# First cross attention: the keys' squares rounded and split by GpSimd, summed by two bf16 matmuls, and taken ahead of the exponential on ScalarE

## The chip, the core and the metric

The kernel runs on one core of a Trainium2 chip. The metric is device time in microseconds of one execution of the whole program, as the median of several runs. The core's engines are TensorE (PE, with PEld for its weight loads), VectorE (DVE), ScalarE (ACT), GpSimd (POOL) and SyncE (SP, which here issues DMAs). Each has its own queue of instructions and runs it in order; semaphores tie the queues together.

## The reference, cut to what matters

The program is a decoder of two layers with a self attention, a cross attention and a feed-forward part each, and a layer norm behind every part. The change touches the cross attention of the first layer only (2 batches, 512 queries and 1024 keys each, 16 heads of 128, model width 512, context width 256):

```python
def _L0_xattn_ref(hidden_states, encoder_hidden_states, Wq, Wk, Wv, Wo, gq, gk):
    def rmsnorm(x, g, eps=1e-05):
        var = jnp.mean(jnp.square(x), axis=-1, keepdims=True)
        return x * jax.lax.rsqrt(var + eps) * g
    q = (hidden_states @ Wq).reshape(B, Sq, H, D)
    k = (encoder_hidden_states @ Wk).reshape(B, Skv, H, D)
    v = (encoder_hidden_states @ Wv).reshape(B, Skv, H, D)
    q = rmsnorm(q, gq)
    k = rmsnorm(k, gk)
    scores = jnp.einsum('bqhd,bkhd->bhqk', q, k) * scale
    attn = jax.nn.softmax(scores, axis=-1)
    out = jnp.einsum('bhqk,bkhd->bqhd', attn, v)
    return out.reshape(B, Sq, H * D) @ Wo
```

The part in question is the sum of a key's 128 squares inside `rmsnorm(k, gk)`.

## The kernel before

All products are float32 in effect: each operand is held as a bf16 high part and a bf16 remainder (hi and lo), and `three` (L1270) multiplies hi by hi, hi by lo and lo by hi into one bank of PSUM. These are the matmuls of L1272, L1273 and L1274 in the profile, whatever they compute; their tiles tell them apart (`k,q` are the scores, `wo,v` the product of probabilities and values, `cT,wkv` with 512 columns the keys, `xT,wq` the queries, `wkv,cT` with 128 columns the values). The transposed probabilities lie in memory that later holds the output weights, so the trace calls them `wo`.

Each attention runs over 32 units, a unit being one head of one batch, and a unit over QT = 4 tiles of 128 queries, in the order of `unit` on each engine. For a tile, TensorE (L1424) makes the scores, then the tile's jobs for the next unit, and then weighs the values for the tile three behind (LAG, L39). VectorE (L1209) scales the scores and finds their maximum (L1191), and later writes the remainder of the normalised probabilities (`remainder`, L1206). ScalarE (L883) writes the rounded probabilities of the tile before (`rounded`, L881), the negated maximum (L890), and the exponential (L892). SP transposes both parts by DMA (L467, L470).

The jobs prepare queries, keys and values of the next unit. Their plan is written out by hand in `Layer.jobs` (L71):

```python
plan = [[("K", 0)], [("KN", 0), ("K", 1)], [("KN", 1), ("Q", 0)], [("QN", 0), ("V", 0), ("V", 1)]]
```

K is a product of half the keys (512 of them), KN the sum of that half's squares, Q the queries, QN the sums of their squares, V half the values. In `job` (L1379) they take turns in two banks of PSUM, so each waits until VectorE is through with the job before the last (`job_lo`, L1384). On ScalarE `job_parts` (L821) takes a K out of PSUM twice behind the tile's exponential: squares into `sq` (L836), then the high part of the scaled keys into `k_hi` (L842). VectorE's part of a K is the low part `k_lo` (L1149), of a KN the scaled sum in `rk` (L1137). KN on TensorE (L1404) is one float32 multiplication of a matrix of ones with `sq`, which the trace shows as two matmuls; it waits for `sq_ok`. `key_norms` (L846) turns the sums into reciprocal roots at the end of the third tile.

GpSimd raises the query norms to the power -1/2 (L651) and splits weights into high and low parts, `split_hi` (L551) and `split_lo` (L556): in units with n % 4 of 2 or 3 the next heads' weights, in the last three units the output weights (`split_wo`). The latter's DMAs wait on SP until earlier pieces are split.

This layer's units are unrolled. Ahead of unit 0 the jobs of "unit -1" run alone, each step waiting for the one before.

Of the kernel before, what the change touches and what calls it, by code (L numbers as in the profile page):

```python
# [23 lines left out]
ALU = mybir.AluOpType  # L24
ACT = mybir.ActivationFunctionType
# [99 lines left out]
def build(nc, a, out, kept):  # L125
    ctx = ExitStack()
    with ctx:
# [19 lines left out]
        rstd = sb("rstd", [P, NT], F32)  # L147
        half_neg = sb("half_neg", [P, QT], F32)
        ones = sb("ones", [P, P], F32)
        idx = sb("idx", [P, IT], I32)  # L150

        q_max, q_inv, q_up, q_scale = (sb(x, [P, 48], F32) for x in ("q_max", "q_inv", "q_up", "q_scale"))
# [31 lines left out]
        t_amax, t_scaled, t_sum, qt_ok, qt_mm, qt_T = (sem(x) for x in ("t_amax", "t_scaled", "t_sum", "qt_ok", "qt_mm", "qt_T"))  # L184
        fg_mm, fu_mm, g_ok, u_ok, fs_ok, fy_ok = (sem(x) for x in ("fg_mm", "fu_mm", "g_ok", "u_ok", "fs_ok", "fy_ok"))

        idb_ok = sem("idb_ok")
        row_in = [sem(f"row_in{i}") for i in range(11)]

        by_name = {L.name: L for L in LAYERS}  # L190
# [65 lines left out]
        for li, L in enumerate(stages):  # L256
# [41 lines left out]
                m["rot"], m["swap"] = sb("rot", [P, 2, S], F32, s), sb("swap", [P, 2, S], F32, s)  # L298
            if L.rms:
                m["sq"] = sb("sq", [P, S], F32, s)  # L300
                m["rk"] = sb("rk", [P, 2, SC], F32, s)
                m["nq"] = sb("nq", [P, 2, QT], F32, s)
                m["g"] = sb("g", [P, 2], F32, s)
                m["mx"] = sb("mx", [P, 2], F32, s)
                m["gg"] = sb("gg", [P, 1], F32, s)
# [223 lines left out]
        def _(pool):  # L529
# [16 lines left out]
            nc.gpsimd.memset(ones[:, :], 1.0).then_inc(const_ok, 1)  # L546
            pool.wait_ge(const_ok, 4)
            nc.gpsimd.tensor_scalar(idb[:, :], ident[:, :], 1.0, 1.0, ALU.mult, ALU.mult).then_inc(idb_ok, 1)

            def split_hi(hi, src):  # L550
                nc.gpsimd.tensor_scalar(hi, src, 1.0, 1.0, ALU.mult, ALU.mult).then_inc(w_hi, 1)  # L551
# [53 lines left out]
            for li, L in enumerate(stages):  # L605
# [39 lines left out]
                def query_norms(n, it, qt, jobs):  # L645

                    for x, (kind, _) in enumerate(jobs):
                        if kind == "QN":
                            pool.wait_ge(job_lo, at(lambda n: c["lo"] + L.before(n, qt) + x + 1, n, it))
                            r = m["nq"][:, (n + 1) % 2, :]  # L650
                            nc.gpsimd.tensor_tensor(r, r, half_neg[:, 0:QT], ALU.pow).then_inc(q_norm, 1)  # L651

                def rope(n, it, qt, jobs):
                    for x, (kind, _) in enumerate(jobs):
                        if kind not in ("K", "Q"):
                            continue
                        r = ("Q", "K").index(kind)
                        hi = lambda n: c["hi"] + L.before(n, qt, BY_ACT) + x + 1
                        lo = lambda n: c["lo"] + L.before(n, qt) + x + 1
                        pool.wait_ge(job_hi, at(hi, n, it))  # L660
                        nc.gpsimd.tensor_tensor(m["swap"][:, r, :], m["swap"][:, r, :], m["sin"][:, :], ALU.mult).then_inc(rope_mul, 1)
                        pool.wait_ge(rope_mul, at(lambda n: c["rope"] + L.rope_count(n, qt) + 1, n, it))
                        pool.wait_ge(job_lo, at(lo, n, it))
                        nc.gpsimd.tensor_tensor(m["rot"][:, r, :], m["rot"][:, r, :], m["swap"][:, r, :], ALU.add).then_inc(rope_sum, 1)
# [6 lines left out]
                def unit(n, it):  # L671
                    for qt in range(QT):
                        if L.rope and qt:
                            rope(n, it, qt, L.jobs(n, qt))
                        if L.rms:
                            query_norms(n, it, qt, L.jobs(n, qt))
                        j, pieces = L.split_plan(n, qt)
                        for kind, part in pieces:
                            if part == 0:
                                pool.wait_ge(w_in[j], at(lambda n: c[f"win{j}"] + (32 if j == 0 or not L.gqa else 16) * (n // 4 + 2), n, it))  # L680
                                pool.wait_ge(job_mm, at(lambda n: c["job"] + L.before(n), n, it))
                                pool.nop(nofuse=True)
                            qkv_piece(L, kind, j, part, at(lambda n: c["whi"] + qkv_item(L, kind, j, n // 4 + 1), n, it))
                        if L.rope and qt == 0:
                            rope(n, it, qt, L.jobs(n, qt))
                        k = QT * (n - UNITS + 3) + qt - 1
                        if 0 <= k < 8:
                            split_wo(k)

                for n in (-2, -1):  # L690
                    for qt in range(QT):
                        if L.rope:
                            rope(n, None, qt, L.jobs(n, qt))
                        if L.rms:
                            query_norms(n, None, qt, L.jobs(n, qt))
                units(pool, unit, L)

# [24 lines left out]
        def _(act):  # L722
# [31 lines left out]
            for li, L in enumerate(stages):  # L754
# [34 lines left out]
                if names[li] == "ffn1":  # L789
# [28 lines left out]
                        turned_rows(t)  # L818
                    continue

                def job_parts(n, it, qt, jobs):  # L821
                    b, u = L.batch(n + 1), n + 1
                    for x, (kind, half) in enumerate(jobs):
# [4 lines left out]
                        if kind == "V":  # L828
                            nc.scalar.activation(m["v"][0][:, L.kvslot(u), 4 * half:4 * half + 4, :], bank.rearrange("p (t d) -> p t d", d=HD), ACT.Copy).then_inc(job_hi, 1)
                        elif L.rope:  # L830
                            r = ("Q", "K").index(kind)
                            nc.scalar.activation(m["swap"][0:64, r, :], bank[64:128, :], ACT.Copy)
                            nc.scalar.activation(m["swap"][64:128, r, :], bank[0:64, :], ACT.Copy).then_inc(job_hi, 1)
                        else:
                            if L.rms:
                                nc.scalar.activation(m["sq"][:, :], bank, ACT.Square).then_inc(sq_ok, 1)  # L836
                            if kind == "Q":
                                nc.scalar.activation(m["q"][0][:, u % 2, :], bank, ACT.Copy).then_inc(job_hi, 1)
                            else:
                                o = m["k"][0][:, L.kvslot(u), half * 512:half * 512 + 512]  # L840
                                if L.rms:
                                    nc.scalar.activation(o, bank, ACT.Copy, scale=m["gg"][:, 0:1]).then_inc(job_hi, 1)  # L842
                                else:
                                    nc.scalar.activation(o, bank, ACT.Copy).then_inc(job_hi, 1)
# [38 lines left out]
                def unit(n, it):  # L883
                    for qt in range(QT):
                        if n or qt:
                            rounded(*((n, it, qt - 1) if qt else (n - 1, it, QT - 1)))
                        act.wait_ge(s_max, at(lambda n: CREDIT + c["s"] + QT * n + qt + 1, n, it))
                        prob = m["p"][:, qt % 2, 0:L.width(qt)]
                        if L.rms:
# [16 lines left out]
                    act.wait_ge(const_ok, 7)  # L906
                for n in (-2, -1):
                    for qt in range(QT):
                        job_parts(n, None, qt, L.jobs(n, qt))
                        if L.rope and (n == -2 or qt == 0):  # L910
                            rotated(n, None, qt)
                        if L.rms:
                            key_norms(n, None, qt, L.jobs(n, qt))
# [355 lines left out]
        def _(pe):  # L1269
# [26 lines left out]
            for li, L in enumerate(stages):  # L1296
# [82 lines left out]
                def job(n, it, qt, x, kind, half):  # L1379
# [20 lines left out]
                            for ch in range(L.chunks):  # L1400
                                last = three(bank[:, t * P:t * P + P], lambda k: src[k][:, ch, o:o + P], lambda k: w(k, 1, ch), ch == 0, ch == L.chunks - 1)
                    elif kind == "KN":
                        pe.wait_ge(sq_ok, at(lambda n: c["sq"] + 3 * (n + 1) + half + 1, n, it))
                        last = nc.tensor.matmul(bank, ones[:, :], m["sq"][:, :], start=True, stop=True)  # L1404
                    elif kind == "QN":
                        pe.wait_ge(sq_ok, at(lambda n: c["sq"] + 3 * (n + 1) + 3, n, it))
                        for q in range(QT):
# [142 lines left out]
```

## Time and profile before

| | us |
|---|---|
| median of 3 runs (2616.11 to 2622.53) | 2621.8 |
| the profiled execution | 2614.38 |
| its span, first to last instruction | 2612.6 |
| TensorE busy | 2438.2 (93%) |
| VectorE busy | 1848.3 (71%) |
| ScalarE busy | 1588.8 (61%) |
| GpSimd busy | 711.8 (27%) |

Busy time counts an engine's instructions from start to end; matmuls overlap one another, so the step from the start of one kind of work to the start of the next says more than their durations. In a timeline the first number is the start in us from the start of the span, the second the duration, then engine, line, operation, tiles written and read, shapes, and in brackets how long the engine stood idle before it and what released it.

### The profile page before, as it was taken

The page shows a single profiled execution, that of the slowest core. Times are in us where ns is not written, and L with a number is a line of the kernel's source. Part 1 is how long each engine was busy: PE and PEld are TensorE (multiplying, and loading weights), DVE is VectorE, ACT ScalarE, POOL GpSimd, SP SyncE. Part 2 cuts the span into 40 slices and gives each one's busy share as a digit, 9 for nine tenths or more (in the row PEclk, how much of TensorE's full clock was granted, in tenths as well). Part 3 has the DMA queues.
Part 4 walks back from the last instruction along what each step waited for, and adds up shares of the span by engine and source line. Part 5 has one row for each costly group of instructions (what it writes and reads, how often), then busy time and mean ns, then how long its engine had stood idle before and what let it go on. Part 6 is the DMA issues. An engine that isn't in the chain of part 4 may idle for free. (4 is left out here: it accounts for less than half of the span.)

```text
span 2612.6 us, 57672 instructions
## 1 busy us (share of the span) xinstructions
PE 2438.2 (93%) x21584; PEld 1567.4 (60%) x21584; DVE 1848.3 (71%) x3371; ACT 1588.8 (61%) x2718; POOL 711.8 (27%) x671
## 2 busy tenths in 40 slices
PE   7999998989999999999988999999899999999864
PEld 4555555546666666666465666665566666665432
DVE  4777777657777777776665666667578888884597
ACT  5777675158887777886244566553277777773242
POOL 5666665601111111012332222226100000013111
PEclk9999999999999999999988999999999999999987
DMA  2433335325666666667341444445188777777200
GB/s 93 90 76 87 79 82 127 103 55 108 114 118 110 113 109 117 115 108 154 113 169 26 94 93 96 95 93 139 30 146 149 145 147 144 146 149 153 69 1 32
DMA packets 769429, 273.83 MB, mean 105 GB/s; under 512 B 737905, under 2 KB 740721, under 8 KB 767601
## 3 DMA queue, kind: packets, MB, share of 16 engines
q1 hardware_dynamic: 767504, 265.82, 49.0%
q0 software_dynamic: 1760, 5.77, 0.8%
q8 instruction: 110, 1.80, 0.3%
q14 instruction: 55, 0.44, 0.1%
HBM read 84.55 MB, written 6.44 MB: 35 GB/s over the span
## 5 line engine op out<-in xcount | busy, mean ns | idle before, releaser
L881 ACT ACTIVATE phl<-p,ri 128x1024 bf16<-128x1024 f32 (+4 forms) x512 | 437.4, 854 | 414.0 <-DVE ri L1196 386.1
L1206 DVE SCALAR_TENSOR_TENSOR phl<-p,ri,phl 128x1024 bf16<-128x1024 f32 (+4 forms) x512 | 514.1, 1004 | 103.3 <-issue 75.3
L892 ACT ACTIVATE p<-p,nb 128x1024 f32<-128x1024 f32 (+4 forms) x512 | 435.9, 851 | 53.9 <-DVE nb L1189 39.6
L1273 PE MATMUL ps<-wo_lo,v_hi 128*128 128x128 bf16 x2496 | 440.0, 220 | 0.0
L1272 PE MATMUL ps<-wo_hi,v_hi 128*128 128x128 bf16 x2240 | 396.5, 220 | 23.0 <-DMA wo_hi<-phl 15.7
L1274 PE MATMUL ps<-wo_hi,v_lo 128*128 128x128 bf16 x2240 | 396.2, 220 | 0.0
L1272 PE MATMUL ps<-k_hi,q_hi 128*128 128x512 bf16 (+3 forms) x768 | 272.5, 355 | 20.9 <-DVE nb L1187 18.7
L1273 PE MATMUL ps<-k_lo,q_hi 128*128 128x512 bf16 (+3 forms) x768 | 271.9, 354 | 0.0
L1274 PE MATMUL ps<-k_hi,q_lo 128*128 128x512 bf16 (+3 forms) x768 | 271.7, 354 | 0.0
L1273 PEld LDWEIGHTS ps<-wo_lo,v_hi 128*128 128x128 bf16 x2496 | 245.1, 98 | 33.4 <-issue 0.5
L1272 PEld LDWEIGHTS ps<-wo_hi,v_hi 128*128 128x128 bf16 x2240 | 219.5, 98 | 68.0 <-DMA wo_hi<-phl 27.9
L551 POOL TENSOR_SCALAR wkv_hi<-raw_kv 128x1024 bf16<-128x1024 f32 (+1 forms) x56 | 49.2, 878 | 658.9 <-PE ps L1274 509.5
L1274 PEld LDWEIGHTS ps<-wo_hi,v_lo 128*128 128x128 bf16 x2240 | 219.7, 98 | 0.0
L1272 PE MATMUL ps<-xT_hi,wq_hi 128*128 128x512 bf16 x512 | 195.1, 381 | 4.5 <-DVE xT_lo L958 3.5
L1191 DVE CUSTOM_DVE_ANT_0 p<-ps,rk,nq 128x1024 f32<-128x1024 f32 x128 | 163.1, 1274 | 51.3 <-PE ps L1274 51.0
L1273 PE MATMUL ps<-xT_lo,wq_hi 128*128 128x512 bf16 x512 | 195.1, 381 | 0.0
L1274 PE MATMUL ps<-xT_hi,wq_lo 128*128 128x512 bf16 x512 | 195.1, 381 | 0.0
L1272 PE MATMUL ps<-wo_hi,oT_hi 128*128 128x512 bf16 x512 | 194.4, 380 | 0.6 <-DVE nb L1187 0.6
L1273 PE MATMUL ps<-wo_lo,oT_hi 128*128 128x512 bf16 x512 | 194.2, 379 | 0.0
L1274 PE MATMUL ps<-wo_hi,oT_lo 128*128 128x512 bf16 x512 | 194.1, 379 | 0.0
L651 POOL TENSOR_TENSOR nq<-nq,half_neg 128x4 f32<-128x4 f32 x32 | 32.3, 1010 | 549.6 <-DVE nq L1140 549.6
L1189 DVE CUSTOM_DVE_ANT_0 p<-ps,mb 128x1024 f32<-128x1024 f32 x128 | 155.8, 1217 | 36.5 <-PE ps L1274 34.2
(200 smaller groups left out, 6126.5 us busy)
## 6 DMA issues: line engine op xcount, KB each, us to landing
raw_kv<-in_wkvself SPq DMA_DIRECT2D x32, 512.0 KB, 4.0
raw_q<-in_wqself SPq DMA_DIRECT2D x32, 256.0 KB, 2.6
raw_q<-in_woself SPq DMA_DIRECT2D x32, 256.0 KB, 2.8
raw_q<-in_wqcross SPq DMA_DIRECT2D x32, 256.0 KB, 3.0
raw_q<-in_wocross SPq DMA_DIRECT2D x32, 256.0 KB, 3.0
wo_hi<-phl SPq DMA_TRANSPOSE x384, 3.2
wo_lo<-phl SPq DMA_TRANSPOSE x384, 3.1
raw_kv<-in_wkvcross SPq DMA_DIRECT2D x24, 256.0 KB, 3.2
```

The source lines that it names most:

```text
L551: nc.gpsimd.tensor_scalar(hi, src, 1.0, 1.0, ALU.mult, ALU.mult).then_inc(w_hi, 1)
L651: nc.gpsimd.tensor_tensor(r, r, half_neg[:, 0:QT], ALU.pow).then_inc(q_norm, 1)
L881: nc.scalar.activation(m["ph"](qt, w), m["p"][:, qt % 2, 0:w], ACT.Copy, scale=ri[:, qt % 2:qt % 2 + 1]).then_inc(p_norm, 1)
L892: nc.scalar.activation(prob, prob, ACT.Exp, scale=1.0 if L.rms else -1.0, bias=nb[:, qt % 2:qt % 2 + 1], accum_out=rs[:, qt % 2:qt % 2 + 1 ...
L1189: ins = nc.vector.tensor_tensor_reduce(in1=m["mb"][:, L.batch(n), :], scale=-ISQ, op0=ALU.add, **kw)
L1191: ins = nc.vector.tensor_tensor_reduce(in1=m["rk"][:, n % 2, :], scale=m["nq"][:, n % 2, qt:qt + 1], op0=ALU.mult, **kw)
L1206: nc.vector.scalar_tensor_tensor(out=m["pl"](qt, w), in0=m["p"][:, qt % 2, 0:w], scalar=ri[:, qt % 2:qt % 2 + 1], in1=m["ph"](qt, w), op0= ...
L1272: nc.tensor.matmul(o, l(0), r(0), start=first, stop=False)
L1273: nc.tensor.matmul(o, l(0), r(1), start=False, stop=False)
L1274: return nc.tensor.matmul(o, l(1), r(0), start=False, stop=last)
```

## The change

ScalarE: the squares of the keys move from `job_parts`, behind the exponential, to a new `key_squares` ahead of the wait for the maximum. GpSimd: a new `squares` rounds `sq` to bf16 (`sqh`) and subtracts to get the remainder (`sql`), in the tiles that have a K, ahead of its other work in that tile. TensorE: KN waits for `sq_lo` and makes two bf16 matmuls with bf16 ones. The squares of the queries stay behind the exponential and now also wait for `sq_lo`.

```diff
@@ build: semaphores and buffers
+        onesb = sb("onesb", [P, P], BF16)
+        idb_ok, onesb_ok = sem("idb_ok"), sem("onesb_ok")
+        sq_hi, sq_lo = sem("sq_hi"), sem("sq_lo")
+                m["sqh"], m["sql"] = sb("sqh", [P, S], BF16, s), sb("sql", [P, S], BF16, s)
@@ GpSimd
+            nc.gpsimd.tensor_scalar(onesb[:, :], ones[:, :], 1.0, 1.0, ALU.mult, ALU.mult).then_inc(onesb_ok, 1)
+                def squares(n, it, qt, jobs):
+                    for kind, half in jobs:
+                        if kind == "K":
+                            pool.wait_ge(sq_ok, at(lambda n: 3 * (n + 1) + half + 1, n, it))
+                            if half:
+                                pool.wait_ge(job_mm, at(lambda n: c["job"] + L.before(n, 1) + 1, n, it))
+                            elif n >= 0:
+                                pool.wait_ge(job_mm, at(lambda n: c["job"] + L.before(n - 1, 2) + 1, n, it))
+                            nc.gpsimd.tensor_scalar(m["sqh"][:, :], m["sq"][:, :], 1.0, 1.0, ALU.mult, ALU.mult).then_inc(sq_hi, 1)
+                            pool.wait_ge(sq_hi, at(lambda n: 2 * (n + 1) + half + 1, n, it))
+                            nc.gpsimd.tensor_tensor(m["sql"][:, :], m["sq"][:, :], m["sqh"][:, :], ALU.subtract).then_inc(sq_lo, 1)
@@ GpSimd, unit and the units ahead of 0
                         if L.rms:
+                            squares(n, it, qt, L.jobs(n, qt))
                             query_norms(n, it, qt, L.jobs(n, qt))
@@ ScalarE
+                def key_squares(n, it, qt, jobs):
+                    for x, (kind, half) in enumerate(jobs):
+                        if kind == "K":
+                            act.wait_ge(job_mm, at(lambda n: c["job"] + L.before(n, qt) + x + 1, n, it))
+                            if n >= 0 or half:
+                                act.wait_ge(sq_lo, at(lambda n: 2 * (n + 1) + half, n, it))
+                            nc.scalar.activation(m["sq"][:, :], ps[:, M_BANK + (L.before(n, qt) + x) % 2, :], ACT.Square).then_inc(sq_ok, 1)
@@ ScalarE, job_parts
-                            if L.rms:
+                            if L.rms and kind == "Q":
+                                act.wait_ge(sq_lo, at(lambda n: 2 * (n + 1) + 2, n, it))
                                 nc.scalar.activation(m["sq"][:, :], bank, ACT.Square).then_inc(sq_ok, 1)
@@ ScalarE, unit
                             rounded(*((n, it, qt - 1) if qt else (n - 1, it, QT - 1)))
+                        if L.rms:
+                            key_squares(n, it, qt, L.jobs(n, qt))
                         act.wait_ge(s_max, at(lambda n: CREDIT + c["s"] + QT * n + qt + 1, n, it))
@@ ScalarE, the units ahead of 0
+                        if L.rms:
+                            key_squares(n, None, qt, L.jobs(n, qt))
                         job_parts(n, None, qt, L.jobs(n, qt))
@@ TensorE, job
                     elif kind == "KN":
-                        pe.wait_ge(sq_ok, at(lambda n: c["sq"] + 3 * (n + 1) + half + 1, n, it))
-                        last = nc.tensor.matmul(bank, ones[:, :], m["sq"][:, :], start=True, stop=True)
+                        pe.wait_ge(onesb_ok, 1)
+                        pe.wait_ge(sq_lo, at(lambda n: 2 * (n + 1) + half + 1, n, it))
+                        nc.tensor.matmul(bank, onesb[:, :], m["sqh"][:, :], start=True, stop=False)
+                        last = nc.tensor.matmul(bank, onesb[:, :], m["sql"][:, :], start=False, stop=True)
```

## Rows read from the trace of the kernel before

**Rows 1.** Busy time by stretch, one unit: stretch, its length, each engine's busy time, clock, DMA.

```profile
826.56:847.74 21.18, 21.09 (x207) 14.30 (x205) 15.70 (x26) 16.94 (x27) 2.02 (x3) 1.00 0.69 125
```

**Rows 2.** Who waited for whom, 560 to 1190 us: total, times, longest.

```profile
DVE k_lo L1149 <- ACT k_hi L842: 58.1, 59, 1.4
...
PEld ps L1272 <- DVE k_lo L1149: 41.6, 59, 1.0
```

**Rows 3.** Timeline of TensorE in that unit, first matmul of each kind of work.

```profile
827.85 0.38 PE L1272 MATMUL ps<-cT_hi,wkv_hi 128*128 128x512 bf16 x1
...
829.15 0.22 PE L1272 MATMUL ps<-wo_hi,v_hi 128*128 128x128 bf16 x1
...
831.78 1.02 PE L1404 MATMUL ps<-sq,ones 128*128 128x512 f32 x2
832.89 0.39 PE L1272 MATMUL ps<-cT_hi,wkv_hi 128*128 128x512 bf16 x1
...
836.84 1.02 PE L1404 MATMUL ps<-sq,ones 128*128 128x512 f32 x2
837.69 0.38 PE L1272 MATMUL ps<-xT_hi,wq_hi 128*128 128x512 bf16 x1
...
840.28 0.22 PE L1272 MATMUL ps<-wo_hi,v_hi 128*128 128x128 bf16 x1
```

**Rows 4.** Timeline of ScalarE in that unit.

```profile
829.52 0.20 ACT L890 ACTIVATE nb<-mx 128x1 f32<-128x1 f32 x1 [0.87 <-DVE mx L1191]
829.75 1.15 ACT L892 ACTIVATE p<-p,nb 128x1024 f32<-128x1024 f32 x1
...
830.90 0.57 ACT L836 ACTIVATE sq<-ps 128x512 f32<-128x512 f32 x1
831.38 0.68 ACT L842 ACTIVATE k_hi<-ps,gg 128x512 bf16<-128x512 f32 x1
...
840.48 0.60 ACT L836 ACTIVATE sq<-ps 128x512 f32<-128x512 f32 x1 [0.26 <-PE ps L1274]
```

**Rows 5.** Timeline of VectorE in that unit.

```profile
829.40 1.28 DVE L1206 SCALAR_TENSOR_TENSOR phl<-p,ri,phl 128x1024 bf16<-128x1024 f32 x1
832.09 0.75 DVE L1149 SCALAR_TENSOR_TENSOR k_lo<-ps,gg,k_hi 128x512 bf16<-128x512 f32 x1 [1.40 <-ACT k_hi L842]
...
834.24 1.28 DVE L1206 SCALAR_TENSOR_TENSOR phl<-p,ri,phl 128x1024 bf16<-128x1024 f32 x1
```

**Rows 6.** Timelines of GpSimd, VectorE and TensorE at places of this and the next stage.

```profile
1191.21 0.62 POOL L551 TENSOR_SCALAR wo_hi<-raw_q 128x512 bf16<-128x512 f32 x1 [4.09 <-DMA raw_q<-in_wocross]
...
1195.16 1.28 DVE L1206 SCALAR_TENSOR_TENSOR phl<-p,ri,phl 128x1024 bf16<-128x1024 f32 x1 [0.49 <-issue]
...
1195.60 1.32 POOL L551 TENSOR_SCALAR wo_hi<-raw_q 128x512 bf16<-128x512 f32 x1 [2.54 <-DMA raw_q<-in_wocross]
1197.01 1.16 POOL L556 TENSOR_TENSOR wo_lo<-raw_q,wo_hi 128x512 bf16<-128x512 f32 x1
...
1211.16 1.42 DVE L1206 SCALAR_TENSOR_TENSOR phl<-p,ri,phl 128x1024 bf16<-128x1024 f32 x1
...
1211.59 2.01 POOL L556 TENSOR_TENSOR wo_lo<-raw_q,wo_hi 128x512 bf16<-128x512 f32 x1
...
1327.42 6.17 POOL L625 TENSOR_TENSOR gu_lo<-oT_hi,gu_hi 128x2048 bf16<-128x2048 f32 x1 [14.94 <-ACT gu_hi L763]
...
1333.65 0.39 PE L1272 MATMUL ps<-xT_hi,gu_hi 128*128 128x256 bf16 x1 [4.99 <-POOL gu_lo L625]
```

**Rows 7.** Entry of the stage: busy time by stretch (as rows 1), then timelines.

```profile
535.00:545.25 10.25, 8.14 (x17) 2.40 (x17) 2.51 (x5) 3.19 (x5) 0.00 (x0) 0.62 0.01 2
...
538.15 0.60 ACT L836 ACTIVATE sq<-ps 128x512 f32<-128x512 f32 x1 [2.32 <-PE ps L1274]
...
538.90 2.04 PE L1404 MATMUL ps<-sq,ones 128*128 128x512 f32 x2 [0.84 <-ACT sq L836]
540.73 0.63 PE L1272 MATMUL ps<-cT_hi,wkv_hi 128*128 128x512 bf16 x1
...
545.25 0.39 PE L1272 MATMUL ps<-xT_hi,wq_hi 128*128 128x512 bf16 x1 [0.18 <-DVE k_lo L1149]
```

More of the change, by code:

```diff
@@ L185, in build @@
         fg_mm, fu_mm, g_ok, u_ok, fs_ok, fy_ok = (sem(x) for x in ("fg_mm", "fu_mm", "g_ok", "u_ok", "fs_ok", "fy_ok"))
-        idb_ok = sem("idb_ok")
+        idb_ok, onesb_ok = sem("idb_ok"), sem("onesb_ok")
+        sq_hi, sq_lo = sem("sq_hi"), sem("sq_lo")
         row_in = [sem(f"row_in{i}") for i in range(11)]
@@ L694, in _ @@
                         if L.rms:
+                            squares(n, None, qt, L.jobs(n, qt))
                             query_norms(n, None, qt, L.jobs(n, qt))
```

## The prediction, made before the changed kernel had run

> **What bounds the kernel now.** I read the busy shares by stretch first, then who waited for whom inside the first cross attention, then one unit of that stage (one head of one batch) engine by engine, then the places where GpSimd works beside VectorE, and last the entry of the stage. The unit that I follow lasts 21.18 us, from its first scores to the next unit's, and TensorE is busy for 21.09 of them (matmuls are pipelined, so a short wait hides in that figure), ScalarE 16.94, VectorE 15.70, GpSimd 2.02 [rows 1]. So TensorE looks like the whole bound. The waits say something finer: TensorE's weight loads stood 41.6 us, 59 times, on VectorE's low half of the keys (k_lo, L1149), and that operation in turn 58.1 us on ScalarE's high half (L842) [rows 2]. In TensorE's rows it is seen at the second key product: the sums of squares start at 831.78 and the next product only at 832.89, 1.11 later, while the second sums (836.84 to 837.69) take 0.85 [rows 3]. The 0.26 between is a wait for k_lo, which starts at 832.09 and lets TensorE go at 832.89, 0.80 later [rows 3, 5]. The second place, Q at 837.69, is held by TensorE itself by a small margin. TensorE and the loop of ScalarE and VectorE are therefore nearly equally long; an edit that shortens one and touches the other must be walked through both.
>
> **The parts, and the price of each.**
>
> Removed: 64 float32 sums (two matmuls each), 0.85 us of TensorE each [rows 3]. Added: 64 pairs of bf16 matmuls. A key product is six of them with 512 columns in 1.30 us (827.85 to 829.15 [rows 3]), so 0.22 each and 0.43 a pair. By itself that frees 0.42 x 2 = 0.84 us a unit, over 31 units and the entry 27 us: the most this change could ever give.
>
> Moved on ScalarE: the key squares now stand ahead of the exponential. A square starts 0.20 after TensorE turns to the next work (840.28 to 840.48), lasts 0.58 to 0.60, and the following operation starts 0.48 after it (830.90 to 831.38) [rows 3, 4]. First key half: TensorE leaves it at 829.15, so square 829.35, negated maximum 829.83 (before 829.52), exponential 0.23 later, 830.06, high keys 1.15 after that, 831.21 (before 831.38: the square now fills part of the idle time ahead of the maximum). k_lo follows 0.71 behind (831.38 to 832.09), at 831.92, and TensorE may start the second product at 832.72 [rows 4, 5].
>
> Added on GpSimd, which has room: a rounding of 128x512 took 0.62, a subtraction 1.16, the second starting 0.09 behind the first [rows 6]. Undisturbed, and with 0.08 for the hand-over from ScalarE too, that would be 829.93 + 0.08 + 0.62 + 0.09 + 1.16 = 831.88, just when TensorE is through its scores at 831.78. But it isn't undisturbed. VectorE's remainder (L1206, both inputs in SBUF) runs from 829.40 to 830.68 [rows 5]. Where GpSimd started within such an operation (1195.60, VectorE 1195.16 to 1196.44), its rounding took 1.32 in place of 0.62 and ended 0.48 behind VectorE; a subtraction at 1211.59 took 2.01 in place of 1.16, beside a remainder that itself took 1.42 in place of 1.28 [rows 6]. So the rounding ends at 830.68 + 0.48 = 831.16, the subtraction runs 831.25 to 832.41, and TensorE starts 0.06 later (a subtraction that ended at 1333.59 released it at 1333.65 [rows 6]), at 832.47. The pair ends at 832.90, and there the second key product starts: 0.01 later than before. The whole 0.42 that TensorE was given, and the 0.26 that it had waited, is spent waiting for GpSimd.
>
> A rule of the skill, in sentences of their own: the Trainium skill ("SBUF — State Buffer", Who interferes with whom) has GpSimd and a VectorE instruction with two SBUF inputs shut each other out for the whole instruction. By it GpSimd's full 0.62 would follow VectorE's end and not 0.48, 0.14 more a unit, 4.3 us over the stage.
>
> Second key half: product 832.90 to 834.20, square 834.40, maximum 834.88 (it could go earlier; ScalarE now waits for TensorE ahead of it), exponential 835.11, high keys 836.26, k_lo 836.97, and Q on TensorE 0.80 later at 837.77, against 837.69: 0.08 late. This step comes out of the order alone: from second product to Q it was 4.80, now it is 1.30 + 0.20 + 0.48 + 0.23 + 1.15 + 0.71 + 0.80 = 4.87. GpSimd here: the remainder stood 2.15 behind k_lo (832.09 to 834.24 [rows 5]), so now 834.07 to 835.35; rounding done at 835.83, subtraction 835.92 to 837.08, sums 837.14 to 837.57, hidden under Q's wait with 0.20 to spare. The second saving of 0.42 is lost as well, to the wait for k_lo.
>
> From Q on TensorE has its own work until the next unit, and nothing there changes; the whole row of events stands 0.08 later. The rest costs nothing: the exponential up to 0.8 us later, since its transposes are used three tiles of queries on; weight splitting in 14 units, now behind the squares' split on GpSimd's queue, whose results are wanted most of a unit later (its last piece can hold up a remainder by some 0.2, hidden behind Q); the wait of Q's square for the split, done 3 us before; no DMA is added and SP's queue issues what it did, with the wo loads of the last three units released in time as no square stands in the third and fourth tile. The one rounding of the ones lies in the kernel's first microseconds, beside the loading.
>
> Entry of the stage: here each step waits for the one before. The first square is at 538.15 and the second product at 540.73, Q at 545.25; over the 10.25 us to there the granted clock was 0.62 on average, that is 1.2 GHz (0.5) up to about 542.8 and 2.4 GHz after (0.5 + 0.5 x 2.46 / 10.25) [rows 7]. Now: square ends 538.75, rounding 538.83, subtraction 539.54 to 540.70, sums (at the lower clock 0.86) 540.76 to 541.62, second product to 543.4, square to 544.2, subtraction to 546.15, sums to 546.6, so Q at 546.6: 1.4 late.
>
> Sum: 31 x 0.08 + 1.4 = **3.9 us slower**. The profiled execution took 2614.38 with a span of 2612.6; it becomes 2618.3. The median shown, 2621.8, lies 7.4 above that execution, and the runs shown spread over 6.4; on the median I put 2625.7.
>
> What no row shows is the hand-over from GpSimd to TensorE in this stage. Lower end 0.06 as above; upper end 0.15, what ScalarE's square needed to start the float32 sums (538.75 to 538.90 [rows 7]); I take 0.06, since it is the same pair of engines. It is also open whether the two engines shut each other out here as they did there: if GpSimd were undisturbed, the second product would start at 832.72 and Q at 837.59, 0.10 early, -3.1 + 1.4 = -1.7 us in all. With the upper hand-over (31 x 0.09 = 2.8), and another 0.14 a unit behind VectorE if the rounding needed its whole 0.62 from there (4.3), it would be 3.9 + 2.8 + 4.3 = +11.
>
> **Rivals.**
> (a) TensorE's time comes through: the 27 us less the entry, some 25 us faster, 2597. For it: TensorE is busy 99.6% of the unit. Against: the 59 waits for k_lo, and that the chain to k_lo isn't shortened but for 0.17 us. It decides if ScalarE's or VectorE's chain is 0.3 shorter at both places than my rows say.
> (b) The clock at the entry. In the new order TensorE does less and stands longer between 538 and 547. If it stays at 1.2 GHz, the second product lasts 2.6 from 541.62, ScalarE and GpSimd need 2.8 behind it, the sums 0.86, and Q starts at 547.9 (2.6 late), takes 5.18 in place of 2.59 (837.69 to 840.28 [rows 3]), and ends 5.2 late; every microsecond of products behind Q at that level adds one more. In place of 1.4 that makes 2.5 + 5.2 = +7.7 us, and +11 with three microseconds more of products: 2629.5 to 2633, slower. It decides whether the clock is still low after 543. For it: the rise at 542.8 followed an unbroken run of matmuls from 538.9, and that run is now broken twice. Against: Q's products come as one block of 2.6 us or more, and no row shows that a break of 2 to 3 us keeps the clock down. The Trainium skill ("TensorE: Matmul & The Clock Gate", What's actually happening) says that the clock is low by default and activity releases it; by that rule sparser work keeps it low longer, which is this case.
> (c) GpSimd later than I have it, through the lock or the hand-over, by over 0.12 us at the first sums: each 0.1 costs 3.1 us, and the upper ends give +11, 2633, also slower.
> (d) GpSimd isn't held up: -1.7, 2620; same.
>
> **How the numbers follow.** A change of under 0.3% (7.9 us) can't be told from none. My forecast (+3.9, with its neighbours (d) and the milder forms of (c)) has 0.70; (a) 0.05; (b) 0.13; (c) beyond the bound 0.10; 0.02 for faster in no named way stays with "same". So faster 0.05, same 0.72, slower 0.23. The range runs from (d) with 2 us for the spread of the runs, 2618, to the upper ends, 2634.
>
> **What would show it.** Right: sums of squares at 0.43 a pair; TensorE idle some 0.7 ahead of the first sums in each unit, released by GpSimd; a rounding of over 0.9 us in each first half; Q released by k_lo; a unit of 21.2 to 21.3 us. Wrong: a unit under 20.9 (rival a), roundings all at 0.62 (d), or Q of the entry with matmuls 0.43 apart (b).

## The result, and the profile after

The changed kernel takes 2626.99 us in the median of 9 runs (2625.09 to 2632.16), the kernel before 2621.8 (9 runs). The ratio is 1.0029, with a 95% interval of 1.0019 to 1.0039 (it isn't the quotient of the two medians, which is 1.0020): slower by 5 to 10 us. That is little, but the interval leaves out no change, and the fastest run after (2625.09) lies above the slowest before (2624.97). The profiled execution took 2627.02 us with a span of 2625.1.

Of TensorE's 27 us of relief not one has reached the end. The page after, busy time and share, shows the relief itself (PE 2438.2 before) and what GpSimd took over (POOL 711.8 before, 671 instructions):

```profile
PE 2405.3 (92%) x21345; PEld 1551.7 (59%) x21584; DVE 1844.7 (70%) x3371; ACT 1589.0 (61%) x2718; POOL 845.4 (32%) x800
```

One unit of the stage, by stretch (columns as in [rows 1]), lasts 21.35 us instead of 21.18, with TensorE busy for 20.46 of them instead of 21.09:

```profile
834.22:855.57 21.35, 20.46 (x205) 13.81 (x206) 15.71 (x26) 16.96 (x27) 5.14 (x5) 1.00 0.64 124
```

TensorE's timeline in that unit, which answers to [rows 3]:

```profile
835.51 0.38 PE L1304 MATMUL ps<-cT_hi,wkv_hi 128*128 128x512 bf16 x1
...
836.80 0.22 PE L1304 MATMUL ps<-wo_hi,v_hi 128*128 128x128 bf16 x1
...
840.20 0.38 PE L1437 MATMUL ps<-sqh,onesb 128*128 128x512 bf16 x1 [0.60 <-POOL sql L667]
840.42 0.38 PE L1438 MATMUL ps<-sql,onesb 128*128 128x512 bf16 x1
840.63 0.38 PE L1304 MATMUL ps<-cT_hi,wkv_hi 128*128 128x512 bf16 x1
...
844.87 0.38 PE L1437 MATMUL ps<-sqh,onesb 128*128 128x512 bf16 x1 [0.15 <-POOL sql L667]
845.09 0.38 PE L1438 MATMUL ps<-sql,onesb 128*128 128x512 bf16 x1
845.50 0.39 PE L1304 MATMUL ps<-xT_hi,wq_hi 128*128 128x512 bf16 x1
```

A pair of sums takes 0.43 (840.20 to 840.63), where the float32 sums took 0.85. From the first key product to the second it is now 5.12 us (835.51 to 840.63); before it was 5.04. From there to Q it is 4.87 (845.50), before 4.80. GpSimd and VectorE in the same unit, which answer to [rows 5, 6]:

```profile
837.69 1.13 POOL L665 TENSOR_SCALAR sqh<-sq 128x512 bf16<-128x512 f32 x1 [5.50 <-ACT sq L846]
838.90 1.16 POOL L667 TENSOR_TENSOR sql<-sq,sqh 128x512 bf16<-128x512 f32 x1
842.81 0.68 POOL L665 TENSOR_SCALAR sqh<-sq 128x512 bf16<-128x512 f32 x1 [2.75 <-ACT sq L846]
```

```profile
837.06 1.28 DVE L1238 SCALAR_TENSOR_TENSOR phl<-p,ri,phl 128x1024 bf16<-128x1024 f32 x1
839.57 0.75 DVE L1181 SCALAR_TENSOR_TENSOR k_lo<-ps,gg,k_hi 128x512 bf16<-128x512 f32 x1 [1.23 <-ACT k_hi L870]
```

The first rounding begins 0.63 into VectorE's remainder (837.06 to 838.34), takes 1.13 instead of 0.62 and ends at 838.82, 0.48 behind it: the number of [rows 6] once more. The subtraction ends at 840.06, and TensorE starts at 840.20, 0.14 later. k_lo, which would have let the product go at 839.57 + 0.80 = 840.37, is no longer what comes last there. ScalarE's timeline has the square ahead of the negated maximum, as walked:

```profile
837.00 0.60 ACT L846 ACTIVATE sq<-ps 128x512 f32<-128x512 f32 x1 [0.70 <-PE ps L1306]
837.50 0.19 ACT L920 ACTIVATE nb<-mx 128x1 f32<-128x1 f32 x1
837.72 1.15 ACT L922 ACTIVATE p<-p,nb 128x1024 f32<-128x1024 f32 x1
...
838.87 0.67 ACT L870 ACTIVATE k_hi<-ps,gg 128x512 bf16<-128x512 f32 x1
```

The waits from 560 to 1190 us (as in [rows 2], where k_lo held the weight loads 41.6 us in 59 waits) say the same in sum:

```profile
PE ps L1437 <- POOL sql L667: 23.8, 49, 1.7
...
PEld ps L1304 <- DVE k_lo L1181: 16.0, 31, 0.6
```

The waits for k_lo are down to 31: 30 stand ahead of Q, one a unit, and one ahead of a second key product, in the first unit of the stretch. The 28 that are gone stood ahead of the second key product, where GpSimd now comes last.

The length of the stage's units can be had from one row: the power of the query norms runs once a unit, first and last start are given, and 31 units lie between. Tile `nq`, before and after:

```profile
L651 POOL TENSOR_TENSOR nq<-nq,half_neg x32: 1006/1009/1020, 550.1 to 1205.3; 128x4 f32<-128x4 f32 x32
```

```profile
L655 POOL TENSOR_TENSOR nq<-nq,half_neg x32: 1017/1018/1027, 555.7 to 1216.0; 128x4 f32<-128x4 f32 x32
```

That is 655.2 us before and 660.3 after: **5.1 us** in the units. More is in the entry. I take it from the last turning matmul of the stage before (a product with the identity, L1278, after the change L1310) to the last matmul of V ahead of unit 0: 19.07 us before (533.48 to 552.55) and 22.72 after (535.48 to 558.20), **3.65 us** more. The spans of the two profiled executions differ by 12.5 us; the other 3.8 lie where the change has no part, 2.0 ahead of the entry and 1.8 behind the last power of the query norms. TensorE's timeline there after the change (compare [rows 7]; steps of 0.43 between 512-column matmuls are the 1.2 GHz level, 0.22 the 2.4 GHz level):

```profile
542.84 0.59 PE L1437 MATMUL ps<-sqh,onesb 128*128 128x512 bf16 x1 [2.78 <-POOL sql L667]
...
543.64 0.63 PE L1304 MATMUL ps<-cT_hi,wkv_hi 128*128 128x512 bf16 x1
...
549.13 0.59 PE L1437 MATMUL ps<-sqh,onesb 128*128 128x512 bf16 x1 [2.72 <-POOL sql L667]
...
549.94 0.63 PE L1304 MATMUL ps<-xT_hi,wq_hi 128*128 128x512 bf16 x1
550.37 0.63 PE L1305 MATMUL ps<-xT_lo,wq_hi 128*128 128x512 bf16 x1
...
551.99 0.38 PE L1306 MATMUL ps<-xT_hi,wq_lo 128*128 128x512 bf16 x1
552.20 0.38 PE L1304 MATMUL ps<-xT_hi,wq_hi 128*128 128x512 bf16 x1
```

TensorE waits 2.8 and 2.7 us for GpSimd, the second key product runs wholly at 1.2 GHz, and the clock rises only within Q, just before 552: it was low from 534.8 to 551.9, where before it was from 532.5 to 542.8. By stretch, the granted clock between 535 and 560 us was 0.84 before and 0.66 after.

### The profile page after: what moved, and what is told of

It reads as the page before. It is cut to its first block and busy times, and to the rows that moved or that the text cites. A ratio compares the mean times of both kernels' runs of the same rounds, so it can differ in the third digit from the quotient of the medians.

```text
span 2625.1 us, 57720 instructions
## 1 busy us (share of the span) xinstructions
PE 2405.3 (92%) x21345; PEld 1551.7 (59%) x21584; DVE 1844.7 (70%) x3371; ACT 1589.0 (61%) x2718; POOL 845.4 (32%) x800
## 5 line engine op out<-in xcount | busy, mean ns | idle before, releaser
L1305 PE MATMUL ps<-k_lo,q_hi 128*128 128x512 bf16 (+2 forms) x767 | 271.4, 354 | 7.1 <-issue 0.4
L1304 PE MATMUL ps<-k_hi,q_hi 128*128 128x512 bf16 (+3 forms) x640 | 223.0, 349 | 22.5 <-DVE nb L1219 20.7
L1223 DVE CUSTOM_DVE_ANT_0 p<-ps,rk,nq 128x1024 f32<-128x1024 f32 x128 | 163.2, 1275 | 51.1 <-PE ps L1306 51.0
L1304 PE MATMUL ps<-wkv_hi,xT_hi 128*128 128x128 bf16 x1024 | 176.2, 220 | 1.1 <-DVE rot L1175 1.1
L1305 PE MATMUL ps<-wkv_lo,xT_hi 128*128 128x128 bf16 x1024 | 176.2, 220 | 0.0
```

What stands on the lines that cost most here:

```text
L1223: ins = nc.vector.tensor_tensor_reduce(in1=m["rk"][:, n % 2, :], scale=m["nq"][:, n % 2, qt:qt + 1], op0=ALU.mult, **kw)
L1304: nc.tensor.matmul(o, l(0), r(0), start=first, stop=False)
L1305: nc.tensor.matmul(o, l(0), r(1), start=False, stop=False)
```

## The experiments

All were compared with the kernel before on the same chip, whose median there was 2618.9 us for the first four, 2616.7 for the next four and 2614.3 for the last; so ratios are to be compared, and not medians. "Unit" is the median distance of the query norms' power from one unit to the next, 21.19 us in the kernel before and 21.35 in the changed one.

**Order alone.** From the changed kernel, with GpSimd's split and the bf16 sums taken out again:

```diff
-                            if n >= 0 or half:
-                                act.wait_ge(sq_lo, ...)
-                            squares(n, it, qt, L.jobs(n, qt))
-                        nc.tensor.matmul(bank, onesb[:, :], m["sqh"][:, :], start=True, stop=False)
-                        last = nc.tensor.matmul(bank, onesb[:, :], m["sql"][:, :], start=False, stop=True)
+                        last = nc.tensor.matmul(bank, ones[:, :], m["sq"][:, :], start=True, stop=True)
```

> Only the order on ScalarE is changed: float32 sums as before, no work for GpSimd. If GpSimd's late split holds the first half (my theory), the second key product starts on k_lo, 0.17 us earlier than in the kernel before, and Q 0.10 earlier: a unit of 21.09 us instead of 21.19, 3 us faster than before over 31 units, entry of the stage as before (clock low for some 10 us). Rival, the order itself costs the time: a unit over 21.2 us, the same as the changed kernel's 21.35 if it is all of it.

Measured: 2618.2 us against 2618.9, ratio 0.9995 (0.9986 to 1.0004); unit 21.11 us. The unit is where my theory had it, and so is the step from the first key product to the second: 4.87 us in the median, 5.04 in the kernel before and 5.12 in the changed one. A saving of 2.5 us is too small for the medians to show. The order doesn't cost the time by itself, so the split does.

**Squares behind the exponential, split kept.**

```diff
-                            key_squares(n, it, qt, L.jobs(n, qt))
...
-                            if L.rms and kind == "Q":
-                                act.wait_ge(sq_lo, at(lambda n: 2 * (n + 1) + 2, n, it))
+                            if L.rms:
+                                if kind == "Q" or half or n >= 0:
+                                    act.wait_ge(sq_lo, at(lambda n: 2 * (n + 1) + (2 if kind == "Q" else half), n, it))
                                 nc.scalar.activation(m["sq"][:, :], bank, ACT.Square).then_inc(sq_ok, 1)
```

> The split on GpSimd and the bf16 sums stay, the squares go back behind the exponential. My theory: the rounding now meets no remainder on VectorE and takes 0.62 us in both halves, but starts so late that the second key product starts 1.1 us later than in the kernel before and Q 0.9 later: a unit of 22.1 us, some 28 us over the stage and 3.6 at the entry, 32 slower than before (2654). Rival, the lock between the two engines is what costs, and not the length of GpSimd's part: without the meeting the unit gets shorter than 21.35.

Measured: 2654.4 us, ratio 1.0141 (1.0123 to 1.0159), which is 37 us (32 to 42); unit 22.11 us, as the theory had it, and not shorter, as the rival would have made it. The roundings of this kernel, minimum, median and maximum in ns, over all 64 of them, and then those of the changed kernel, of which 60 met a remainder:

```profile
L665 POOL TENSOR_SCALAR sqh<-sq x64: 619/619/627, 540.5 to 1230.3; 128x512 bf16<-128x512 f32 x64
```

```profile
L665 POOL TENSOR_SCALAR sqh<-sq x64: 617/914/1477, 540.8 to 1206.2; 128x512 bf16<-128x512 f32 x64
```

The same instruction takes 0.62 us wherever it doesn't meet a remainder. But undisturbed or not, GpSimd's chain (0.62 + 1.16 and the hand-overs) costs what it ends behind its need: begun behind the exponential, where nothing disturbs it, it makes the unit 0.76 us dearer than in the changed kernel. Moving the squares ahead was what made the split nearly free.

**One bf16 sum, no remainder.** The remainder of the squares is left out of the sum:

```diff
-nc.scalar.activation(m["sq"][:, :], ps[:, M_BANK + ...], ACT.Square)
+nc.scalar.activation(m["sqh"][:, :], ps[:, M_BANK + ...], ACT.Square)
...
+                        last = nc.tensor.matmul(bank, onesb[:, :], m["sqh"][:, :], start=True, stop=True)
```

> Leaves the squares' remainder out: ScalarE writes the key squares as bf16 alone, ahead of the exponential, and TensorE sums them in one matmul; GpSimd has no part in it. TensorE has 1.27 us less to do in each unit than in the kernel before. My theory, that ScalarE and VectorE's chain to k_lo decides: a unit of 21.09 us as with the order alone, 3 us faster than before, and the entry within 3 us of the one before. Rival, TensorE's work decides: a unit of 19.9 us, 39 us faster.

Measured: 2617.8 us, ratio 0.9994 (0.9984 to 1.0004); unit 21.11 us, to 0.001 us that of the order alone, with 1.27 us less work for TensorE. Its second key product:

```profile
855.14 0.38 PE L1432 MATMUL ps<-sqh,onesb 128*128 128x512 bf16 x1
856.09 0.39 PE L1299 MATMUL ps<-cT_hi,wkv_hi 128*128 128x512 bf16 x1 [0.56 <-DVE k_lo L1176]
```

The sum would be over 0.22 after its start; the product comes 0.95 after it, released by k_lo. This is the plainest proof that, with the keys' high part behind the exponential, TensorE's work on the sums isn't what the unit waits for.

**The wait for the split first.**

```diff
+                    if kind == "KN":
+                        pe.wait_ge(sq_lo, at(lambda n: 2 * (n + 1) + half + 1, n, it))
                     pe.wait_ge(job_lo, at(lambda n: c["lo"] + L.before(n, qt) + x - 1, n, it))
...
-                        pe.wait_ge(onesb_ok, 1)
-                        pe.wait_ge(sq_lo, at(lambda n: 2 * (n + 1) + half + 1, n, it))
```

The wait for the ones (`onesb_ok`) now stands once, ahead of the stage.

> The changed kernel with the wait for the split as the first wait of the sums, so that it may ride on the weight load itself and not on an instruction of its own ahead of it. Theory: the hand-over from GpSimd to TensorE falls from 0.14 us to 0.05 to 0.06, the unit from 21.35 to 21.27, 2.5 us faster than the changed kernel (2624.5). Rival, the 0.14 is the two engines' own and the order of waits means nothing: 21.35.

Measured: unit 21.28 us; 2625.8 us, ratio 1.0029 (1.0015 to 1.0043), as the changed kernel, 2 us being below what medians resolve. The hand-over: a subtraction from 836.58 for 1.16, and the load that it released.

```profile
836.58 1.16 POOL L667 TENSOR_TENSOR sql<-sq,sqh 128x512 bf16<-128x512 f32 x1
...
837.79 0.10 PEld L1437 LDWEIGHTS ps<-sqh,onesb 128*128 128x128 bf16 x1 [1.00 <-POOL sql L667]
837.80 0.39 PE L1437 MATMUL ps<-sqh,onesb 128*128 128x512 bf16 x1 [0.51 <-POOL sql L667]
```

It is 0.06 us now instead of 0.14, and so throughout: 0.05 to 0.06 in all 64 hand-overs of this kernel, 0.14 to 0.15 in all 64 of the changed one. What each weight load waited for, in the changed kernel and here, from 560 to 1190 us:

```profile
PEld ps L1437 <- issue: 51.8, 59, 2.1
```

```profile
PEld ps L1437 <- POOL sql L667: 51.7, 60, 2.1
```

In the changed kernel the wait for GpSimd stands on an instruction of its own ahead of the load, so the load itself is released by nothing that the profile names. The edit also takes a wait away (that for the ones), but their number isn't the cause: the float32 sums of the kernel before had two waits too, with the wanted one second, and stood 0.14 to 0.15 behind ScalarE's square. In these kernels the order in which the program writes its waits decides which of them rides on the instruction.

**Keys' high part ahead as well, float32 sums.** On top of the order alone:

```diff
                             nc.scalar.activation(m["sq"][:, :], ..., ACT.Square).then_inc(sq_ok, 1)
+                            nc.scalar.activation(m["k"][0][:, L.kvslot(n + 1), half * 512:half * 512 + 512], ps[:, M_BANK + (L.before(n, qt) + x) % 2, :], ACT.Copy, scale=m["gg"][:, 0:1]).then_inc(job_hi, 1)
...
-                        if kind not in BY_ACT:
+                        if kind not in BY_ACT or (L.rms and kind == "K"):
```

> Float32 sums as before and no GpSimd; on ScalarE both the key squares and the high part of the keys stand ahead of the exponential. Theory: the kernel before is held at one place only, the wait for k_lo ahead of the second key product (0.26 us a unit); with k_lo 1.3 us earlier this wait is gone, TensorE's own work is all that is left, and the unit falls to 20.92 us, 8 us faster than before. Rival, the later exponential (0.9 us) comes back in the scores or transposes: 21.1 or more.

Measured: 2605.5 us, ratio 0.9946 (0.9934 to 0.9958); unit 20.92 us. The sums and the product behind them:

```profile
849.56 1.02 PE L1432 MATMUL ps<-sq,ones 128*128 128x512 f32 x2
850.42 0.38 PE L1300 MATMUL ps<-cT_hi,wkv_hi 128*128 128x512 bf16 x1
```

0.86 apart, with no wait. It is clearly faster than the kernel before without any bf16 sum.

**The same, and the second half's sum split.** The split, and the bf16 pair with its wait first, for `half` of 1 and n from 0 only, with the counts waited for to match; all else as above:

```diff
-                        if kind == "K":
+                        if kind == "K" and half:
...
+                        if n < 0 or not half:
+                            pe.wait_ge(sq_ok, at(lambda n: c["sq"] + 3 * (n + 1) + half + 1, n, it))
+                            last = nc.tensor.matmul(bank, ones[:, :], m["sq"][:, :], start=True, stop=True)
+                        else:
```

> As e5_keys_ahead, and only the second half's squares are split by GpSimd and summed in bf16 (that half's split has room: it is wanted 2.6 us behind its square and nothing but a remainder's last 0.3 us stands in its way); first half and entry of the stage in float32. Theory: k_lo no longer hides the second saving of 0.42 us: a unit of 20.50 us, 21 us faster than before. Rival, VectorE or ScalarE is the bound by now: 20.9 as in e5_keys_ahead.

Measured: 2599.7 us against 2616.7, ratio 0.9927 (0.9914 to 0.9940), the fastest kernel of the study; unit 20.68 us, not 20.50. GpSimd and TensorE:

```profile
850.70 0.62 POOL L665 TENSOR_SCALAR sqh<-sq 128x512 bf16<-128x512 f32 x1 [8.08 <-ACT sq L843]
851.40 1.16 POOL L667 TENSOR_TENSOR sql<-sq,sqh 128x512 bf16<-128x512 f32 x1
```

```profile
852.62 0.39 PE L1440 MATMUL ps<-sqh,onesb 128*128 128x512 bf16 x1
```

The expectation counted the 2.6 us of room from the square, but TensorE's other work, which is that room, begins 0.20 ahead of it, where the product ends (849.82 to 850.02). Even undisturbed, square, rounding, subtraction and hand-overs end 2.80 behind the product (849.82 to 852.62), and TensorE's other work lasts only 2.63. So 0.17 of the second 0.42 is lost to GpSimd, and the rest comes through.

**Entry in float32.** The changed kernel with the sums ahead of unit 0 as before (and the counts waited for to match):

```diff
+                        if n < 0:
+                            pe.wait_ge(sq_ok, at(lambda n: c["sq"] + 3 * (n + 1) + half + 1, n, it))
+                            last = nc.tensor.matmul(bank, ones[:, :], m["sq"][:, :], start=True, stop=True)
+                        else:
...
-                            squares(n, None, qt, L.jobs(n, qt))
```

> The changed kernel with the sums ahead of unit 0 left in float32 as before. Theory: the units stay at 21.35 and the entry is that of the kernel before, with the clock low for some 10 us and not 17: 3 us faster than the changed kernel, 5 slower than before. Rival, the length of the low clock at the entry has to do with the moment at which the stage begins and not with the split: no faster than the changed kernel, and the entry as long as its own.

Measured: unit 21.35 us as expected. In its profile the entry (last turning matmul to last matmul of V) took 18.6 us instead of 22.7, and the granted clock from 535 to 560 was 0.86 instead of 0.66. The median, 2623.2 us, ratio 1.0025 (1.0013 to 1.0037), can't be told from the changed kernel's 1.0029. But every profile has an entry. With the split in it, it took 22.7, 21.5, 22.7, 22.8 and 21.9 us (changed kernel, squares behind, wait first, and the two below), mean 22.3; without it 19.1, 20.7, 20.1, 19.2, 19.2 and 18.6 (kernel before, order alone, one sum, keys ahead, second half, and this one), mean 19.5. The two sets don't overlap: in the mean the split costs 2.8 us at the entry.

How long the clock stays low is only in part a matter of the split, and there the rival has a point. Order alone and this kernel run the same float32 entry; the clock was at 1.2 GHz for 13.7 us in the one (538.3 to 551.9) and for 6.8 in the other (536.1 to 542.9), and their entries differ by 2.1 us. So a single pair of entries, such as 18.6 and 22.7, doesn't price the split.

**Keys ahead with both sums split.** The two edits of "wait first" and "keys ahead" on the changed kernel.

> e4_wait_first with the high part of the keys also ahead of the exponential: k_lo is early in both halves, so what is left to hold the first half is GpSimd alone. Theory: the second key product still starts 0.01 to 0.05 us later than in the kernel before (GpSimd's rounding waits for VectorE's remainder), the second saving comes through to Q, and the unit is 20.9 us. Rival, GpSimd's part hardly matters once k_lo is early: both savings come through, 20.4.

Measured: 2613.7 us, ratio 0.9980 (0.9970 to 0.9990); unit 20.93 us. With k_lo early, GpSimd alone holds the first half: the scores ahead of the first sums start at 852.56, the sums at 854.52, where 853.85 would do. The first saving is lost still: from the first key product to the second it is 5.04 us in the median, as in the kernel before. Of the second, 0.26 of 0.42 comes through (second product to Q 4.54 instead of 4.80), as in the kernel with only the second half split; the same 0.17 is lost to GpSimd. Where only the second half is split, the unit is 20.68, so splitting the first half costs 0.25 us a unit, even with k_lo early.

**A remainder with one operand.** VectorE's remainder leaves out the subtraction of the high part:

```diff
+                    if L.rms:
+                        nc.vector.tensor_scalar(m["pl"](qt, w), m["p"][:, qt % 2, 0:w], ri[:, qt % 2:qt % 2 + 1], 1.0, ALU.mult, ALU.mult).then_inc(p_lo, 1)
+                        return
```

> The changed kernel, but VectorE's remainder in this stage reads one SBUF operand in place of two: the subtraction of the high part is left out of it (the low part of the probabilities is written as their rounded value). Theory: what holds GpSimd up is the remainder's second operand in SBUF; without it the roundings take 0.62 us in both halves, GpSimd is ready 0.5 us earlier, and the second key product starts on k_lo: a unit of 21.10 us in place of 21.35, 8 us faster than the changed kernel. Rival, any long SBUF operation of VectorE shuts GpSimd out: first-half roundings stay over 0.62 us (unless it ends sooner), and the unit stays above 21.2.

Measured: 2618.1 us against 2614.3, ratio 1.0012 (1.0003 to 1.0022); unit 21.11 us. Its roundings, and one of its remainders:

```profile
L665 POOL TENSOR_SCALAR sqh<-sq x64: 617/617/947, 537.5 to 1195.3; 128x512 bf16<-128x512 f32 x64
```

```profile
851.95 0.75 DVE L1239 TENSOR_SCALAR phl<-p,ri 128x1024 bf16<-128x1024 f32 x1
```

The wait for GpSimd is gone; the unit is that of the order alone, to the hundredth. So the meeting costs 0.24 us a unit, 7.4 us over the stage, in the changed kernel. The ratio says less: 1.0012 against the changed kernel's 1.0029, with intervals that touch.

But the theory of the second operand is wrong. In nearly all first halves the rounding starts 0.63 behind the remainder's start, which lasts only 0.75 now (851.95 in the row above, the rounding 852.58), so it is nearly over. In three places the two still met earlier, and there GpSimd was held up as before:

```profile
958.15 0.95 POOL L665 TENSOR_SCALAR sqh<-sq 128x512 bf16<-128x512 f32 x1 [5.50 <-ACT sq L846]
```

```profile
957.87 0.75 DVE L1239 TENSOR_SCALAR phl<-p,ri 128x1024 bf16<-128x1024 f32 x1
```

This rounding took 0.95 and ended at 959.10, again 0.48 behind the remainder's end (958.62); the two others (984.20 and 1195.34) ended 0.47 and 0.48 behind. So the form with one operand shuts GpSimd out as well, as the rival had it, and the unit is shorter because the remainder ends sooner.

## Why the prediction was right

It forecast 3.9 us more, and "same" with a lean to slower; measured were 5.2 between the medians and 7.6 by the ratio (5.0 to 10.2). That "same" holds is by a hair, and in part luck: I had set 0.3% as the least that can be told from none, the ratio is 0.29%, and its interval leaves out no change. Both terms of the sum were too small. Point by point:

- **TensorE isn't the bound at the sums.** Right, and shown twice: 1.27 us less of its work changed nothing (one bf16 sum), and 0.26 us of wait for k_lo was all that came of leaving the sums as they are (keys ahead, 21.19 to 20.92). Rival (a) is out.
- **The rounding ends 0.48 behind VectorE's remainder.** Right to 0.01, in all 60 meetings of the changed kernel, and with it the second key product follows GpSimd and not k_lo. My upper end had the whole 0.62 there, which is also what follows from the rule of the Trainium skill ("SBUF — State Buffer", Who interferes with whom) that I quoted; the measurement decides for 0.48. Rival (d), GpSimd undisturbed, is what the one-operand kernel shows, and at 21.11 us a unit it is where (d) had it (21.09). The kernel with one operand also corrects what I took to matter, that both inputs of the remainder lie in SBUF: the form with one input held GpSimd up in the same way.
- **The hand-over to TensorE.** Here the sum was mis-sized: I took 0.06, "since it is the same pair of engines", and it was 0.14, the upper end. It isn't the pair of engines that decides but the place of the wait. Written behind another wait it became an instruction of its own, here as in the float32 sums of before; written first it is 0.06. This is 0.08 x 31 = 2.5 us, and it brings the 2.5 that I had for the units to 5.0, against 5.1 measured. By it the unit, 21.35, also lies just above the 21.2 to 21.3 that I had named as a sign of being right.
- **From the second product to Q, 4.87.** Measured 4.87. The second saving was lost to k_lo as described; with k_lo early 0.26 of its 0.42 come through.
- **The entry.** This term was mis-sized too: I had 1.4 late; it is 2.8 in the mean of the profiles and 3.65 in the one after. The waits for GpSimd came as walked, but rival (b) came half true: the clock stayed at 1.2 GHz through the second product and into Q, and rose just before 552 and not at 543. The first five of Q's twelve matmuls stood 0.43 apart, which I had named as a sign of being wrong. Against my walk, by steps of 0.43 in place of 0.22, this is an estimated 2.1 us in this trace (0.79 in the second product, 0.38 in the second sums, 0.97 in Q), and with the 1.4 it gives 3.5. I had given (b) 0.13 and priced it only in full, at +7.7 in all. That this is close to the ratio's 7.6 is chance: its parts were 2.5 and 5.2, where 5.1 and 2.8 were measured. The rule of the Trainium skill that I quoted there ("TensorE: Matmul & The Clock Gate", What's actually happening), that the clock is low until activity releases it, agrees with this trace: 17.1 us low where TensorE stood twice for 2.8, against 10.2 before. The other traces show that it isn't all: 13.7 us in order alone, where nothing of GpSimd's is waited for, and 13.7 in wait first, with breaks of 2.7 and 2.6.
- **What costs nothing.** Right as far as the trace shows: the weight pieces behind the split, the wo loads, the later exponential and Q's square have left no new wait in the lists.

With the two terms as measured the sum is 5.1 + 2.8 = 7.9 us, inside the interval of the ratio. Together they had fallen short by 3.9 us, the hand-over by 2.5 and the entry by 1.4, well within the range.

What stays open: by the ratio, keys ahead and the one with its second half split gain 14 and 19 us (11 and 17 between the medians), but in the profiles their stage, from the last turning matmul to the last power of the query norms, gains 9.4 and 14.5. The rest of the program, in which the edits have next to no part, took anything from 1938 to 1950 us in the eleven profiled executions, so single executions can't settle this. What share the clock has in the 2.8 us of the entry is open as well.

## What to carry to other kernels

Before work is taken off the busiest engine, look at what releases it at the place where the work ends: here a product that stood 0.26 us for VectorE told that 0.42 of savings would buy nothing, and that moving one 0.68 us copy ahead of a 1.15 us exponential would buy more than 64 cheaper sums. Work moved to an idle engine cost its latency here, and not its time; what counts is how long before its use it can start, and beside which operation it will run. Split only where the result is wanted later than that (the second half here), and leave the entry of a stage, where nothing hides it, as it was.

## What the runs showed of the hardware beside this

- The wait that the program writes first ahead of a matmul rides on the weight load and lets it go 0.05 us behind GpSimd's end; the ones written after it become an instruction of their own in front, and the matmul starts 0.14 us behind (0.06 and 0.14 to 0.15 in all 64 hand-overs of wait first and of the changed kernel). In 31 units that was 2.2 us in the profiles (660.3 to 658.1).
- A rounding on GpSimd (0.62 us alone) that started within VectorE's remainder ended 0.48 us behind it, in all 60 meetings of the changed kernel, whether it had started 0.28 or 1.09 us into it. The remainder with one SBUF operand did the same in three meetings (0.47 to 0.48). VectorE's reading of the scores from PSUM (L1223) did not: the 15 roundings of GpSimd that began beside it in the changed kernel took 0.62.
- VectorE's remainder in this stage took 1.28 us with two SBUF operands and 0.75 with one, for the same 1024 elements.
- At the entry TensorE's clock was at 1.2 GHz for 17.1 us in the changed kernel's trace, with two breaks of 2.8 us in its work and blocks of about 3 us between them, and for 10.2 in that of the kernel before [rows 7]. But the same code doesn't repeat it: the float32 entry of order alone and of entry in float32 had 13.7 and 6.8 us of it, and that of wait first 10.2, then 3.4 us at 2.4 GHz, then 3.4 low again.
